# The first sequence's operands split on VectorE, its weights split product by product, and its first keys gathered from ScalarE's queue

## What is computed

```python
qkv = (x @ w_qkv).reshape(b, s, 3, N_HEADS, HEAD_DIM)
q, k, v = jnp.moveaxis(qkv, 2, 0)
scores = jnp.einsum('bqhd,bkhd->bhqk', q, k) * SCALE
attn = jax.nn.softmax(scores, axis=-1)
out = jnp.einsum('bhqk,bkhd->bqhd', attn, v).reshape(b, s, d)
return out @ w_proj + b_proj          # then: layer norm, experts, layer norm
```

## Time and profile before

| what | us |
|---|---|
| median of 3 runs | 3288.73 |
| the profiled execution, whole | 3292.01 |
| its span in the trace | 3290.2 |
| PE / DVE / ACT / POOL busy in it | 3016.0 / 2546.1 / 2222.5 / 1606.6 |
| first scores matmul (L701) starts at | 49.72 |
| last load of a sequence's x issued (L457) | 1802.9 |
| first matmul of the experts | 2011.38 |

### The profile page before, as it was taken

How to read it: one execution, slowest core, us unless ns; L and a number is a source line. 1 busy time by engine, 2 the same in 40 slices (tenths; PEclk the granted TensorE clock), 3 DMA queues, 4 the chain that set the end, 5 groups by cost and what they waited for, 6 DMA issues and landing times. The chain is left out here.

```text
span 3290.2 us, 63511 instructions
## 1 busy us (share of the span) xinstructions
PE 3016.0 (92%) x21035; PEld 1937.8 (59%) x21035; DVE 2546.1 (77%) x5828; ACT 2222.5 (68%) x4280; POOL 1606.6 (49%) x1412
## 2 busy tenths in 40 slices
PE   4999999999999999999999985999999999999950
PEld 3444444444444445444444434888888888888840
DVE  3788888888887888888888856666666766666769
ACT  2788887888877888788887753555656665556630
POOL 5365655656555565565655421333333333333333
PEclk8999999999999999999999987999999999999975
DMA  3454555433333343333333316877777777777859
GB/s 92 133 166 156 177 159 174 144 85 103 86 99 87 79 109 84 97 92 79 108 85 97 82 45 148 161 159 156 156 154 156 154 160 161 157 157 152 169 154 319
DMA packets 412529, 435.23 MB, mean 132 GB/s; under 512 B 223016, under 2 KB 313520, under 8 KB 412208
## 3 DMA queue, kind: packets, MB, share of 16 engines
q1 hardware_dynamic: 356432, 346.76, 42.6%
q0 software_dynamic: 51168, 67.68, 9.6%
q10 hardware_dynamic: 4608, 16.78, 1.3%
HBM read 183.93 MB, written 146.15 MB: 100 GB/s over the span
## 5 line engine op out<-in xcount | busy, mean ns | idle before, releaser
L1020 DVE TENSOR_REDUCE peak<-ps 128x1 f32<-128x512 f32 x2048 | 1339.1, 684 | 290.4 <-PE ps L701 290.1
L799 ACT ACTIVATE probs<-ps 128x512 f32<-128x512 f32 x2048 | 1124.3, 611 | 172.7 <-PE ps L711 161.5
L1288 POOL DMA_INDIRECT x<-out,token x270 | 435.1, 1611 | 749.7 <-ACT out L1363 628.4
L711 PE MATMUL ps<-stack 50*128 50x512 f32 x2048 | 785.5, 453 | 3.5 <-DVE peak L1020 2.8
L701 PE MATMUL ps<-stack 48*128 48x512 f32 x2048 | 750.8, 444 | 19.9 <-DMA stack<-qk_lo 13.8
L1302 PE MATMUL ps_hid<-x_hi,stack 128*128 128x512 f32 (+1 forms) x2304 | 691.7, 384 | 41.5 <-DVE x_lo L1403 29.5
L701 PEld LDWEIGHTS ps<-stack 48*128 48x128 f32 x2048 | 335.0, 188 | 466.0 <-issue 218.9
L727 PE MATMUL ps_pv<-probs,v 128*17 128x512 f32 x4096 | 546.2, 605 | 1.2 <-ACT probs L799 1.2
L1302 PEld LDWEIGHTS ps_hid<-x_hi,stack 128*128 128x128 f32 x2304 | 422.1, 190 | 130.7 <-issue 43.2
L551 POOL DMA_INDIRECT expert_rows<-row,slot x256 | 254.1, 993 | 404.4 <-DVE token L1000 320.0
L1302 PE MATMUL ps_hid<-x_lo,stack 128*128 128x512 f32 (+1 forms) x1152 | 441.4, 383 | 0.0
(11 more groups left out here) (178 smaller groups left out, 4353.8 us busy)
## 6 DMA issues: line engine op xcount, KB each, us to landing
stack<-qk_hi SPq DMA_DIRECT2D x1024, 64.0 KB, 2.2
expert_rows<-blank SPq DMA_DIRECT2D x81, 520.0 KB, 3.9
probs<-in_L_ffn_W SPq DMA_DIRECT2D x144, 256.0 KB
probs<-in_L_ffn_W SPq DMA_DIRECT2D x72, 512.0 KB, 5.9
raw_odd<-in_L_ffn_W SPq DMA_DIRECT2D x144, 256.0 KB, 4.5
stack<-qk_lo SPq DMA_DIRECT2D x512, 64.0 KB, 2.2
quarters<-expert_rows SPq DMA_DIRECT2D x252, 128.0 KB, 6.2
xs<-in_L_attn_x SPq DMA_DIRECT2D x32, 512.0 KB, 4.3
```

What stands on the lines that cost most here:

```text
L711: pe.matmul(ps[it.bank(("cols", n))][:], k_stack[g][part, h, t * P:(t + 1) * P], q_stack[g][part, h, :], start=True, stop=True).then_inc(s ...
L799: act.activation(probs[:, j % RING, :], ps[it.bank(("cols", s * UNITS + j))][:], ACT.Exp, scale=SCALE).then_inc(s_exp, 1)
L1020: dve.tensor_reduce(peak[s % 2][:, u:u + 1], ps[it.bank(("rows", n))][:], AX.X, ALU.max, negate=True).then_inc(s_max, 1)
L1288: pool.indirect_dma_start(x1_dram, bass.IndirectOffsetOnAxis(ap=token[n % 2][:, t:t + 1], axis=0), out[n % 2][:, t, :], None, bounds_check ...
```

## The change

- `s_w_in` is a semaphore of `w_in`'s load alone; `s_weights` counts the other three, and PE, POOL wait for 48.
- PE takes `xT` of sequence 0 first, as soon as x and the constants are there. The gate rows are transposed in `ps_pv` ahead of `qk0`, and each `qk` product waits for its own weights only (`s_wqk` 2n + 2), `v0` for 10.
- DVE's weight split is cut in five, one for each product and one for the values, and stands between new steps on DVE that do for sequence 0 what POOL did: the split of x, and the sum and split of each product. The constants come before the last product.
- The products' order is q of groups 0, 1, then k of 0, 1, then q and k of 2, 3 (`QK_BLOCKS`), for all sequences. So for sequence 0 the stacks of groups 0 and 1 wait for `s_lo` 2 (`2 * (g // 2) + 2`), not 4. For later sequences the wait stays at 4 per sequence.
- The six key DMAs of group 0 of sequence 0 are issued by ACT (`first_keys`), ahead of its copies of `qk3`.

```diff
-            sp.dma_start(w_in[:], w_qkv.rearrange("(k p) n -> p k n", p=P)).then_inc(s_weights, 16)
+            sp.dma_start(w_in[:], w_qkv.rearrange("(k p) n -> p k n", p=P)).then_inc(s_w_in, 16)
...
-                        sp.wait_ge(s_lo, (b + off) * 4 + 4)
-                        if it.known and b + off == 0:
+                        first_seq = it.known and b + off == 0
+                        sp.wait_ge(s_lo, 2 * (g // 2) + 2 if first_seq else (b + off) * 4 + 4)
+                        if first_seq:
                             sp.wait_ge(s_pad, 2 * g + 2)
...
+                                if first_seq and g == 0:
+                                    continue
+                                sp.dma_start(k_stack[g][rows].bitcast(F32),
+                                             c[part, 2 * m + 1, :].bitcast(F32)).then_inc(s_stack[g], 16)
...
-                if it.on(1):
+                if it.on(1) and b >= 0:
                     for n in range(KT):
                         wait_emptied(pool, s_free, it.emptied("xT"))
...
-            pe.wait_ge(s_weights, 64)
             pe.wait_ge(s_const, 8)
...
-            pe.wait_ge(s_gate, 2)
-            pe.wait_ge(s_wqk, 2)
-            pe.wait_ge(s_zero, 2)
...
+                        if b < 0:
+                            pe.wait_ge(s_weights, 48)
...
                         pe.wait_ge(s_xlo, (b + 1) * KT + KT)
+                    if b < 0:
+                        pe.wait_ge(s_wqk, 2 * n + 2)
...
+                def first_keys():
+
+                    act.wait_ge(s_lo, 2)
+                    act.wait_ge(s_pad, 2)
+                    for half_ in range(2):
+                        part = slice(half_ * (GP // 2), (half_ + 1) * (GP // 2))
+                        for r, c in enumerate((qk_hi[0], qk_hi[0], qk_lo[0])):
+                            rows = slice(HALF * half_ + HD * r, HALF * half_ + HD * (r + 1))
+                            act.dma_start(k_stack[0][rows].bitcast(F32), c[part, 1, :].bitcast(F32)).then_inc(s_stack[0], 16)
...
+                    if name == "qk3" and b < 0:
+                        first_keys()
                     act.wait_ge(s_full, it.full(name))
...
+                for hi, raw in zip(parts(w_qk_hi), raws()):
+                    last = dve.tensor_copy(hi, raw)
+                last.then_inc(s_wqk, 1)
+                dve.wait_ge(s_wqk, 2 * n + 1)
+                for lo, hi, raw in zip(parts(w_qk_lo), parts(w_qk_hi), raws()):
+                    last = dve.tensor_tensor(lo, raw, hi.bitcast(F32), ALU.subtract)
+                last.then_inc(s_wqk, 1)
...
+                if b < 0:
+                    for n in range(KT):
+                        wait_emptied(dve, s_free, it.emptied("xT"))
+                        dve.tensor_copy(x_t_hi[:, n, :], x_t[:, n, :]).then_inc(s_xhi, 1)
+                        dve.wait_ge(s_xhi, n + 1)
+                        dve.tensor_tensor(x_t_lo[:, n, :], x_t[:, n, :], x_t_hi[:, n, :].bitcast(F32),
+                                          ALU.subtract).then_inc(s_xlo, 1)
...
+                    split_weights(0)
+                    split_weights(1)
+                    split_weights(2)
+                    split_qk(0)
+                    split_weights(3)
+                    split_qk(1)
+                    split_value_weights()
+                    split_qk(2)
+                    dve_constants()
+                    split_qk(3)
```

More of the change, by code:

```diff
@@ L33 @@
 UNITS = HG * TILES
+QK_BLOCKS = (0, 2, 1, 3)
 ALL = GROUPS * UNITS
@@ L828, in _, with split_weights, parts @@
             dve.memset(gate_t[:], 0.0).then_inc(s_zero, 1)
-            dve.wait_ge(s_weights, 64)
-            def split_weights(part):
-                for m in range(4):
+            def split_weights(n):
+                def parts(w):
                     for g in range(2):
                         for k in range(KT):
[L836 to L841, removed]
@@ L851, in _, with raws @@
-            for i in range(2):
-                dve.memset(v[i][:, :, :, HD:HD + 1], 1.0)
-            dve.memset(ps_pv[:], 0.0)
-            dve.memset(carry[:], 0.0)
-            dve.memset(count[:, 0, :], 0.0).then_inc(s_zero, 1)
+                            yield w[:, k, n, g * GP:(g + 1) * GP].rearrange("p (a r h) -> p a r h", a=2, h=PAIRS)
+                def raws():
+                    for g in range(2):
+                        for k in range(KT):
+                            first = QK_BLOCKS[n] * P + g * GP
+                            yield w_in[:, k, first:first + GP].rearrange("p (h a r) -> p a r h", h=PAIRS, a=2)
@@ new lines, in split_weights, with split_value_weights @@
+                if n == 0:
+                    dve.wait_ge(s_w_in, 16)
+                for hi, raw in zip(parts(w_qk_hi), raws()):
[5 more added lines that the diff above has]
+                last.then_inc(s_wqk, 1)
+            def split_value_weights():
+                raw = w_in[:, :, 2 * DIM:]
+                dve.tensor_copy(w_v_hi[:], raw).then_inc(s_wqk, 1)
+                dve.wait_ge(s_wqk, 9)
+                dve.tensor_tensor(w_v_lo[:], raw, w_v_hi[:].bitcast(F32), ALU.subtract).then_inc(s_wqk, 1)
@@ new lines, in dve_constants @@
+            def dve_constants():
+                dve.wait_ge(s_gate, 1)
+                dve.wait_ge(s_zero, 1)
+                dve.tensor_copy(gate_t[:, :, 0:EXPERTS],
+                                ps_pv[:, 0:KT * EXPERTS].rearrange("p (k e) -> p k e", k=KT)).then_inc(s_gate, 1)
+                dve.wait_ge(s_gate, 2)
+                for i in range(2):
+                    dve.memset(v[i][:, :, :, HD:HD + 1], 1.0)
+                dve.memset(ps_pv[:], 0.0)
+                dve.memset(carry[:], 0.0)
+                dve.memset(count[:, 0, :], 0.0).then_inc(s_zero, 1)
```

35 lines of the change are left out of this document (20 added, 15 removed).

## The result

The changed kernel took 3264.15 us in the median of 6 runs (3259.36 to 3274.99) against 3288.65 of 6 runs of the kernel before: a ratio of 0.9926, 95% interval 0.9913 to 0.9939, which is 24.5 us. The forecast was 3267 and 21.3 us. The profiled execution has a span of 3258.4 against 3290.2. The experiments ran on three chips, e1 to e4, e5 to e8 and e9 to e12, each time with the kernel before beside them, so they are compared by the ratio to it and not by their microseconds.

The account below looks back on a forecast made before the run. PE, busy 92% of the span, bounds the kernel, so the start-up chain's shift counts: third pair 51.13 - 29.85 = 21.3 us, carried unreduced. 3292.0 less 21.3 is 3270.7, less 3.3 for the median gives 3267.4; range 3257 to 3279.

Parts of the forecast that it names:

- product 0: Sign at the start of sequence 0: the first product would start at 10 to 12 us, against 22.89 before.
- the bound of 17 to 25 for the third pair: Sign at the third scores pair: the prediction is wrong if it is not 17 to 25 us earlier.
- the first pair: Sign at PE's first scores matmuls: they would start at 25 to 27 us, against 49.72 before.
- the nearer range of the third: Sign at the third scores pair: it would come 20 to 22.5 us before the old 51.13.
- The chain to the gather: From x's landing through DVE's splits to the second product's split: group 0 can be gathered at 20.0 against 40.1.
- The lock's 0.65 on x: At DVE's split of x: its casts wait for POOL's pads on the shared port, 0 to 2.0 us, taken as 0.65.
- The gather on two queues: Group 0's 12 stack DMAs, six each on SP and ACT: all in at 25.7 us, 24.0 earlier than 49.72.
- the issue: ACT's six key DMAs: about 635 ns each as on SP, ending at 23.95 us, ahead of the copies of qk3.
- the landing: Group 0's stacks: at a DMA share of 0.41 two queues have room; in 2.3 us after the last issue.
- What is late next: The second pair's bank, held by v1's second half: v1's copies end at 28.6 us, so the third pair runs at 29.85.
- POOL's cover of 1.1: Sequence 1: POOL ends its split of x at 36.1 us, PE's next qk0 is due at 37.2; thinnest cover, 1.1.
- The clock: Rival in the first 120 us: fewer stretches at PE's lower clock level give 4 to 7 us more, 3257 to 3263; chance 0.13.

Follow-up runs that it names:

- e1: The changed kernel with group 0's six key DMAs back on SP, none issued by ACT: 3272.94 us, ratio 0.9935 to the kernel before.
- e4: The changed kernel with DVE splitting all weights in one piece ahead of x: 3267.46 us, ratio 0.9918 to the kernel before.
- e5: The changed kernel with POOL's pads of groups 1 to 3 held until the second product is split: single time 3274.83 us.
- e8: e1 with 22 extra matmuls keeping PE busy while it waits for the stacks: 3279.10 us, ratio 0.9956 to the kernel before.
- e9: e8 with two waits on POOL for its own last result, around xb: one time, 3268.39 us.
- e12: The kernel of e6 again, now timed: 3264.53 us in the median of 6, ratio 0.9920 to the kernel before.
- e3: The changed kernel with POOL splitting x and sequence 0's products as before, DVE only the weights: 3276.56 us, ratio 0.9948 to the kernel before.
- e6: The changed kernel with ACT issuing the six keys behind its copies of qk3, not ahead: single time 3262.79 us.
- e7: The changed kernel with late pads, three keys on ACT behind qk3's copies and three on SP: 3270.47 us, ratio 0.9927 to the kernel before.
- e10: e7 with the two POOL waits of e9: 3270.09 us, ratio 0.9933 to the kernel before.
- e11: The changed kernel itself, unaltered, run again on another chip: 3270.01 us, ratio 0.9939 to the kernel before.
- e2: e1 with the old product order and all stacks waiting for all four products: 3275.77 us, ratio 0.9950 to the kernel before.

## Why the prediction was right, and where it was not

The forecast of the time was right, and in the changed kernel the lead at the third pair, 18.9, is about the lead at the last load, 21.1, and the gain of the timed runs, 24.5 and 21.0. That it goes through unreduced, as the prediction said, is not how it went: it lost 2.0 and won 3.7 on the way, and in other runs single events took 3 to 7 us. That 21.3 came out so nearly is luck. Of the signs set down beforehand, product 0, the first stack DMA and the bound of 17 to 25 for the third pair held; the transposes of x (4.73 for 4.3 to 4.5), the first pair (29.50 for 25 to 27), the second (31.05 for 28 to 30) and the nearer range of the third (18.9 for 20 to 22.5) did not.

*The chain to the gather* was right: x at 4.73 for 4.35, product 0 at 11.51 for 11.0, the first stack DMA at 20.36 for 20.05. The lock's 0.65 on x was 0.26 (0.57 and 0.53 for 0.42 twice), but the first four weight casts took 0.83 more than free; e5 took all of it away and gained 1.2.

*The gather on two queues* is the step that failed, in two terms. The first is the issue: 635 ns for each of ACT's six, 3.9 in all. They took 6.05, and with the start 0.36 late that is the 2.5 us by which `qk3`'s copies were late (26.46 for 23.95) and, nearly, the 2.35 by which the third pair was (32.20 for 29.85). In e3, with no instruction packet in the stretch, the six took 4.15, so the 635 was near and what stretched them was not in the sum. The second is the landing: from a share of 0.41 the prediction said that two queues have room and had the stacks in 5.65 us after the first issue. They took 8.6 in e6 and e3, where PE waited for them, with the engines at 0.78 (22:24 of e6) and 1.06. The prediction had set beside this the rule of the Trainium skill, "DMA: Bandwidth & Descriptors", that a second queue does not help bandwidth, with a gain of 20.0 by it. The 8.6 against the 9.4 to 9.9 of SP alone bear the rule out nearly; it was a mistake to judge the load of two queues by the share of one.

*What is late next* was named rightly: the second pair's bank behind `v1`'s copy. `v1`'s matmuls, which the sum had as covered, ran to 29.5 and held the first pair (29.50 for 25.7), but not the third; in e1, where ACT has no issues ahead, PE waits for the stacks alone, as this says.

*POOL's cover of 1.1* stayed: POOL ended its split of x at 38.4 and PE's `qk0` of sequence 1 started at 39.56, both 2.3 to 2.4 later than forecast, 18.9 before the old 58.49 and waiting for DVE. Nothing was lost there.

*The clock* was a rival of its own and came about, both ways. First a loss. The start of PE's second product of sequence 1 and DVE's reduction after it, from the timelines of 40:50, the changed kernel first and then e1:

```profile
44.39 0.80 PE L647 MATMUL ps<-x_t_hi,w_qk_hi 64*128 64x512 f32 x2
...
47.78 0.69 DVE L1057 TENSOR_REDUCE peak<-ps 128x1 f32<-128x512 f32 x1 [2.08 <-PE ps L710]
...
43.76 0.50 PE L645 MATMUL ps<-x_t_hi,w_qk_hi 64*128 64x512 f32 x2
...
45.70 0.69 DVE L1053 TENSOR_REDUCE peak<-ps 128x1 f32<-128x512 f32 x1 [0.49 <-PE ps L708]
```

In 44:46 the granted clock is 0.50 in the changed kernel and 1.00 in e1, and DVE waits 2.08 for 0.49. Here the lead falls by 1.5, in the changed kernel and in e5, e6, e7, e10 and e11, whose clock is 0.50 to 0.65 there; it does not in e1, e8, e9 and e12, at 1.00, nor in e2, e3 and e4, where these products come later, with the clock back at 1.00. Then a gain. Between the loads of 2 and 3 the lead rises with the clock in 80:120 (last column of the table): by nothing at 0.83, as before (e2, e3, e10), by 2.5 to 3.0 at 0.91, by 3.7 to 4.0 at 0.96 and by 5.0 at 1.00. A clock of 0.96 for 0.83 is some 10 us less at the lower level, an estimate from the two means, so 10 us cost 3.7 here, the upper end of the price that the prediction gave. No run set the clock there by itself; the two go together in all 13 profiles beside that of the kernel before. So what was lost at the keys and at 44 to 48 us was about given back, for a reason that the sum did not have.

A second such place is the load of 19: 5.4 us longer than other sequences in the kernel before too, and 8 to 9 in e3, e4 and e8, whose clock in 1020:1060 is 0.83 for 0.91.

*The parts.* At the third pair: POOL's splits on DVE 6.8 us (e3), two products before the gather 6.0 (e2 against e1), weights by product 4.1 (e4), keys on ACT -0.5 (e1). They are not additive. That x no longer waits for the weights and the gate was not tried alone.

*Open.* The experts' stage took 1152 to 1159 us from first to last matmul in 14 profiles with the same instructions, the last stage 91 to 97 between its stores. The changed kernel's two profiles have 1153.1 and 1152.4, the one of before 1158.0. Whether the change has a part in that can't be told from one profile of before.

## What to carry to other kernels

A cut in a start-up chain arrives at the end about in full, if the steady part waits on nothing but its own chain; here single events moved the lead by 2 to 7 us either way. Find a mark that recurs (a load, once per item) and compare it along the whole run, since this shows in one profile what timed runs with 10 us of spread can't, and where a lead is won or lost. Before putting half of a gather on a second queue, look at the DMA share with the first alone: at 0.4 the second doubled it and saved about 1 of 9 to 10 us, and the copies behind the issues on that engine paid. When an issue is long, don't stop at the DMA share: find a stretch with the same share and short issues, and look at the other queues. And a tiny operation on VectorE can cost what GpSimd has in line, not what it takes itself.

## What the runs showed of the hardware

- SP and ACT together issuing SBUF to SBUF DMAs of 64 KB brought the share of the 16 DMA engines to 0.92 at 175 GB/s (1.06 at 154 in e3). Twelve such DMAs were in after 8.6 to 8.9 us (e3, e6, e12), with SP alone after 9.4 to 9.9 (e1, e2, before).
- An issue takes 0.6 us and now and then 1.1 to 1.9. The long ones overlap packets of the queues called "instruction" (55 of 60 on SP in the changed kernel, against 152 of 1470 shorter ones). At a share of 1.06 without such a packet they stayed at 0.6 (e3).
- A DVE subtraction of 16 columns stood for 3.82 us beside three POOL instructions in line, in 3 of 12 profiles; in the other nine, and in e9 and e10 with waits between them, the longest is 0.94 to 0.96. Four of 64 columns took 3.07 for 0.63 beside POOL's split of x (e3). Beside POOL's memsets only the casts were held (e5).
- 10 us less at the lower level of PE's clock in 80:120 went with a gain of 3.7 us. At 28 to 35 us, where DVE set the pace, it gave 0.3 (e8).
- A sequence takes 58.5 us in steady state, within 0.3 from one to the next; what changes a lead by 3 to 7 us is single events, a held DVE instruction or a stretch at the lower level, in the same kernel in one execution and not in another (e6 and e12).
